# Edge stage of a graph network layer: segment sum in high and low parts, the power on GpSimd, indices made ahead

## The chip, the core and the metric

The kernel runs on one core of a Trainium2 chip. The metric is the device time of one execution in microseconds. Five engines work side by side and meet at semaphores: TensorE (PE, its weight loads as PEld), VectorE (DVE), ScalarE (ACT), GpSimd (POOL) and SyncE (SP), which only issues DMAs here. Each engine takes its instructions in order; a wait holds everything that is queued behind it on that engine.

## The reference

3125 nodes with 256 features, 103125 edges (50000 drawn ones in both directions, and a loop per node), sorted by node. The input is layer-normalized to h, then for every edge

```python
x = concat(h[ei], h[ej], d2)
msg = silu(x @ mW1 + mb1)
msg = layer_norm(msg, ln_g, ln_b)
msg = silu(msg @ mW2 + mb2)
agg = segment_sum(msg, ei, num_segments=3125)
y = silu(concat(h, agg) @ uW1 + ub1) @ uW2 + ub2
```

and behind it, per node, h + y is added to the input, and a feed-forward layer with a routed choice of half of the nodes follows (the node stage, which the change doesn't touch).

## The kernel before

Three stages follow one another, each a block of its own in which all engines start and end together. The first (to about 428 us) sorts edges into 834 tiles of 128 edges, each of which belongs to one of 25 blocks of 125 nodes, and makes `a_sb` (the first layer's part that belongs to the node ei, in a high and a low fp32r part), `b_table` in DRAM (the part of ej, one row per node), and `rec`, a record per edge with the node's place in its block and the neighbour's number in two digits (64 times one plus the other). The third is the node stage (from 1986.84 us).

The edge stage between them works on pairs of tiles: 417 pairs. It is a software pipeline. Slot t of each engine works on pair t in one step, pair t-1 in the next, and so on to pair t-14 (LAST). Six slots are one round; rounds 3 to 68 run as a hardware loop on every engine, those before and behind are written out (`filling`, `draining`).

- **GpSimd**, slot t: two gathers of 128 rows from `b_table` into `g_rows` (L902). It waits for the activation of pair t-6, whose buffer they take (RING is 6), and for the indices that VectorE makes two slots ahead (L1046).
- **SP**, every three slots: `loc_rows` and the lower rows of `ohT` (L877, L880), after TensorE has used the old ones. After the written-out rounds it issues seven loads for the node stage, x among them (L885, L886), before it goes on.
- **VectorE**, slot t, in this order: two additions of `psG` into the block of `agg` of pair t-14 (L1055; the second waits for the first), one-hot `ohT` of pair t-1 (L1139), indices of pair t+2 (L1046), one-hot `ohf` of pair t-12 (L1147), `psH` added to `g_rows` for pair t-2 (L1155), batch statistics of pair t-4 (L1162). Between them, once per three pairs, stand sixteen steps on 6 columns that make the inverse root of the variance by Newton's method and `shift` (L1070 to L1118). At a round's start it loads twelve block numbers into registers (L1042).
- **TensorE**, slot t: `psH` of pair t-2 (L990, fp32r, four matmuls), `psG` of pair t-13 (L999, fp32, the one-hot `ohf` by `msg`), four transposes of `normed` of pair t-10 (L1008), second matmul of pair t-11 into `ps2` (L1016, fp32). One fp32 matmul of 256 columns with 128 rows is two instructions.
- **ScalarE**, slot t: `normed` of pair t-9 (L939, two), Silu of pair t-3 (`act1`, L946), Silu of `ps2` of pair t-12 (`msg`, L951), copy of the transposed ones of pair t-10 (L955).

When GpSimd is through with the gathers it adds h and the bias to x in SBUF (L922, L926, ten instructions).

## Time and profile before

| | |
|---|---|
| median of 3 runs | 2271.79 us (2271.46 to 2272.17) |
| profiled execution: time, span | 2270.75 us, 2268.9 us |
| PE busy | 1973.4 us (87%) |
| DVE busy | 1948.0 us (86%) |
| ACT busy | 1295.1 us (57%) |
| POOL busy | 1035.7 us (46%) |
| gathers (L902) | 834 of 0.948 us |

Times in the views count from the span's start. In a timeline a row is a run of like instructions: its start, its length (up to the end of the last), engine, line, operation, what it writes and reads, the count, and in brackets the idle time of the engine before it with what ended it. Instructions of VectorE overlap: the next one starts before the record of the last ends, so the cost of one is read from start to start. A `q` behind an engine's name marks its sequencer, which issues, waits, branches and loads registers.

### The profile page before, as it was taken

What the parts mean: (1) busy time and instruction counts of PE and PEld (TensorE: products, weight loads), DVE (VectorE), ACT (ScalarE), POOL (GpSimd) and SP (SyncE); (2) the same over time, 40 slices, a digit from 0 to 9 for tenths busy, and PEclk for the clock granted to TensorE, in tenths of its full rate; (3) what the DMA queues carried; (4) which work ended last, traced back from release to release, by engine and by line L of the source; (5) the groups of instructions that cost most, each with busy time, mean ns of one, the idle gap of its engine ahead of it and who ended that gap; (6) DMA issues with size and microseconds to landing.
All of it is one profiled execution on the core that took longest, in us unless ns stands there. A gap on an engine that the chain in (4) does not pass through costs nothing. (4 is left out here: it accounts for less than half of the span.)

```text
span 2268.9 us, 48446 instructions
## 1 busy us (share of the span) xinstructions
PE 1973.4 (87%) x11037; PEld 1678.5 (74%) x11038; DVE 1948.0 (86%) x6373; ACT 1295.1 (57%) x2495; POOL 1035.7 (46%) x1038
## 2 busy tenths in 40 slices
PE   3546674269999999999999999999999997799996
PEld 2324553258888888888888888888888886677775
DVE  5899999659999999999999999999999999746795
ACT  1112331257777777777777777777777775433331
POOL 8753222445555555555555555555555556203000
PEclk9987876579999999999999999999999999899998
DMA  3000000343333333333333333333333333010001
GB/s 123 0 1 21 28 25 18 106 155 91 90 91 97 90 91 97 90 91 97 90 91 97 90 91 97 91 91 97 92 91 97 91 91 73 1 40 2 27 1 57
DMA packets 88779, 164.64 MB, mean 73 GB/s; under 512 B 23133, under 2 KB 59322, under 8 KB 88477
## 3 DMA queue, kind: packets, MB, share of 16 engines
q0 software_dynamic: 42016, 111.40, 18.6%
q1 hardware_dynamic: 45448, 51.78, 7.1%
q10 hardware_dynamic: 1266, 0.83, 0.1%
q8 instruction: 27, 0.44, 0.1%
q14 instruction: 22, 0.18, 0.0%
HBM read 152.30 MB, written 11.65 MB: 72 GB/s over the span
## 5 line engine op out<-in xcount | busy, mean ns | idle before, releaser
L902 POOL DMA_INDIRECT g_rows<-b_table,idx_pair x834 | 790.8, 948 | 704.5 <-DVE idx_pair L1046 566.2
L1016 PE MATMUL ps<-w2g,nT 128*128 128x256 f32 x3336 | 790.8, 380 | 0.0
L1016 PEld LDWEIGHTS ps<-w2g,nT 128*128 128x128 f32 x3336 | 602.9, 191 | 65.0
L939 ACT ACTIVATE normed<-act,shift,rstd_e 128x255 f32<-128x255 f32 x834 | 452.6, 593 | 274.0 <-DVE shift L1118 273.8
L1055 DVE TENSOR_TENSOR agg<-psG,agg 125x256 f32 x834 | 349.4, 419 | 123.3 <-PE psG L999 80.8
L999 PE MATMUL psG<-msg,ohf 128*125 128x256 f32 x1668 | 435.4, 383 | 0.0
L990 PE MATMUL psH<-a_sb,ohT 128*128 x1668 | 344.2, 329 | 67.6 <-issue 47.8
L990 PEld LDWEIGHTS psH<-a_sb,ohT 128*128 128x128 f32 x1668 | 258.6, 192 | 97.4 <-issue 76.1
L946 ACT ACTIVATE act<-g_rows 128x512 f32<-128x512 f32 x417 | 262.8, 630 | 106.1 <-DVE g_rows L1155 94.3
L1162 DVE BATCH_NORM_STATS2 stat_e<-act 128x6 f32<-128x256 f32 x834 | 310.6, 415 | 0.0
L999 PEld LDWEIGHTS psG<-msg,ohf 128*125 128x125 f32 x1668 | 283.7, 187 | 33.9 <-issue 2.2
L1155 DVE TENSOR_TENSOR g_rows<-psH,g_rows 128x512 f32<-128x512 f32 x417 | 284.9, 683 | 6.9 <-DMA g_rows<-b_table,idx_pair 4.7
L955 ACT ACTIVATE nT<-psM 128x512 f32<-128x512 f32 x417 | 247.5, 593 | 56.4 <-PE psM L1008 56.2
L1008 PE MATMUL psM<-identf,normed 128*128 128x128 f32 x1668 | 252.0, 274 | 0.6 <-ACT nT L955 0.6
L951 ACT ACTIVATE msg<-ps 128x512 f32<-128x512 f32 x417 | 241.5, 579 | 5.2 <-PE ps L1016 5.2
L1008 PEld LDWEIGHTS psM<-identf,normed 128*128 128x128 f32 x1668 | 209.6, 141 | 44.1 <-issue 1.3
L1147 DVE TENSOR_TENSOR ohf<-nodes,rec 128x250 f32<-128x250 f32 x417 | 173.4, 416 | 0.0
L1139 DVE TENSOR_SCALAR ohT<-loc_rows,node_col 125x256 fp32r<-125x256 bf16 x417 | 150.3, 361 | 26.4 <-DMA loc_rows<-loc_d 26.1
L512 POOL DMA_INDIRECT rec_d<-recw,dest x62 | 59.7, 962 | 177.5 <-ACT recw L349 83.8
L594 PE MATMUL psK<-oqv,or_ 128*128 128x96 bf16 x806 | 55.7, 232 | 80.6 <-DVE oqv L741 80.6
L349 ACT ACTIVATE recw<-psK 128x96 bf16<-128x96 f32 x62 | 15.4, 250 | 178.4 <-PE psK L594 151.8
L732 DVE TENSOR_TENSOR or_<-x_all,psV 128x1664 bf16<-128x1664 f32 x62 | 116.4, 1877 | 0.0
(200 smaller groups left out, 2150.5 us busy)
## 6 DMA issues: line engine op xcount, KB each, us to landing
loc_rows<-loc_d SPq DMA_DIRECT2D x139, 187.5 KB
g_rows<-b_table,idx_pair POOLq DMA_INDIRECT x834, 2.8
h_sb<-in_x SPq DMA_DIRECT2D x1, 3125.0 KB
b_table<-b_out SPq DMA_DIRECT2D x25, 125.0 KB
x_all<-in_x SPq DMA_DIRECT2D x1, 3125.0 KB
out<-x_all SPq DMA_DIRECT2D x5, 625.0 KB
ohT<-ew_d SPq DMA_DIRECT2D x139, 9.0 KB
rec_d<-rec SPq DMA_DIRECT2D x1, 1668.0 KB, 8.5
```

The source lines that it names most:

```text
L902: pool.indirect_dma_start(g_rows[:, j, n, :], None, b_table[:, :], bass.IndirectOffsetOnAxis(ap=idx_pair[:, j, n:n + 1], axis=0)).then_inc ...
L939: ins = nc.scalar.activation(normed[:, (j - 9) % 2, n, 0:D - 1], act1[:, (j - 9) % RING, n, 0:D - 1], ACT.Identity, scale=rstd_e[:, 1 - fa ...
L946: nc.scalar.activation(act1[:, (j - 3) % RING, :, :], g_rows[:, (j - 3) % RING, :, :], ACT.Silu).then_inc(s_act1, 1)
L951: nc.scalar.activation(msg[:, j % 2, :, :], ps2[:, j % 2, :, :], ACT.Silu).then_inc(s_msg, 1)
L955: nc.scalar.activation(nT[:, j % 2, :, :, :], psM[:, :, :, :], ACT.Copy).then_inc(s_nT, 1)
L990: mm = pe.matmul(psH[:, j % 2, n, :], ohT[:, k, n, :], rows, start=(part == 0), stop=(part == 1))
L999: mm = pe.matmul(psG[0:NB, k, n, :], ohf[:, k, n, :], msg[:, k, n, :], start=True, stop=True)
L1008: mm = pe.transpose(psM[:, n, q, :], normed[:, j % 2, n, q * P:(q + 1) * P], identf[:, :])
L1016: mm = pe.matmul(ps2[:, k, n, :], nT[:, k, n, q, :], w2g[:, q, :], start=(q == 0), stop=(q == 1))
L1055: V.tensor_tensor(room, psG[0:NB, j % 2, n, :], room, ALU.add).then_inc(s_agg, 1)
L1155: V.tensor_tensor(g_rows[:, k, :, :], psH[:, j % 2, :, :], g_rows[:, k, :, :], ALU.add).then_inc(s_hid, 1)
L1162: ins = V.bn_stats(stat[:, q // 3, 2 * (q % 3) + n, :, :].rearrange("p h w -> p (h w)"), act1[:, q, n, :])
```

## The change

- **Segment sum.** `msg` in fp32 is replaced by two fp32r parts. ScalarE writes Silu(`ps2`) as `high` in fp32r, and then Silu(`ps2`) again, in fp32, over `ps2` itself in PSUM; VectorE subtracts to get `low` in fp32r. `psG` is `ohf` (now fp32r) by `high` plus `ohf` by `low`, two matmuls for each tile where there was one fp32 one.
- **Power.** Of the Newton steps five remain, the variance, with `mean2` and `moment` in PSUM. The power -1/2 is one GpSimd instruction (`root`) for three pairs, after the gathers of every third slot, two slots behind the variance; VectorE makes `shift` at the start of the same slot number. ScalarE's steps stand a slot later than before, and so do those behind them; LAST is 15.
- **Indices.** They are made for all tiles at the end of the first stage, three instructions for each of seven groups in place of one copy. In the loop SP copies six columns of them into `idx_ring` for each half round, after the gathers of the round before; the written-out rounds read them in place.
- **Loads.** The seven loads for the node stage are issued by ScalarE, after the written-out rounds, instead of by SP.

```diff
-LAST = 14
+LAST = 15
@@ hand-over
-                    V.tensor_copy(rec[:, g * P:g * P + n, 0:3],
-                                  psR[:, g % 2, :, 0:n].rearrange("p n t -> p t n")).then_inc(s_rec, 1)
+                    link(V.tensor_copy(low_part[:, g * P:g * P + n], psR[:, g % 2, 2, 0:n]))
+                    V.scalar_tensor_tensor(out=idx_all[:, g * P:g * P + n], in0=psR[:, g % 2, 1, 0:n], scalar=64.0,
+                                           in1=low_part[:, g * P:g * P + n], op0=ALU.mult, op1=ALU.add)
+                    V.tensor_copy(loc_e[:, g * P:g * P + n], psR[:, g % 2, 0, 0:n]).then_inc(s_rec, 1)
@@ SP
                         if not has(first, 0):
                             continue
+                        own = bass.ds(2 * first, RING)
+                        if not isinstance(d, int):
+                            for k in range(h * (RING // 2), (h + 1) * (RING // 2)):
+                                sp.wait_ge(s_gather[k], 32 * d)
+                            sp.dma_start(idx_ring[:, h, :], idx_all[:, own]).then_inc(s_idx_in[h], 16)
                         need(sp, s_first, first - RING // 2)
...
                 filling(body)
-                for to, frm in todo:
-                    sp.dma_start(to, frm, allow_slow_non_contiguous=True).then_inc(s_late, 16)
-                sp.dma_start(x_sb[:, :, :], x_v).then_inc(s_xin, 16)
@@ GpSimd
+                def root(d, j):
+                    g, par = (2 * d - 3, 1) if j < 3 else (2 * d - 2, 0)
+                    pool.wait_ge(s_var, 5 * g + 5)
+                    pool.sem_inc(s_apart_pool, 1)
+                    pool.tensor_tensor(rstd_e[:, par, :], var_e[:, par, :], exph[:, 0:6], ALU.pow).then_inc(s_root, 1)
...
                         need(pool, s_act1, t - RING + 1)
-                        pool.wait_ge(s_idx, t + 1)
+                        if not isinstance(d, int) and j % 3 == 0:
+                            pool.wait_ge(s_idx_in[j // 3], 16 * (d - PEEL + 1))
...
+                    if j % 3 == 0 and has(t, 9):
+                        root(d, j)
@@ ScalarE: normed t-10, then
+                    if has(t, 13):
+                        act.wait_ge(s_second, t - 12)
+                        need(act, s_sum, t - 14)
+                        nc.scalar.activation(high[:, (j - 13) % 2, :, :], ps2[:, (j - 13) % 2, :, :], ACT.Silu).then_inc(s_high, 1)
+                    if has(t, 4):
...
-                        nc.scalar.activation(msg[:, j % 2, :, :], ps2[:, j % 2, :, :], ACT.Silu).then_inc(s_msg, 1)
+                    if has(t, 13):
+                        act.wait_ge(s_high, t - 12)
+                        nc.scalar.activation(ps2[:, (j - 13) % 2, :, :], ps2[:, (j - 13) % 2, :, :], ACT.Silu).then_inc(s_msg, 1)
...
                 filling(body)
+                for to, frm in todo:
+                    act.dma_start(to, frm, allow_slow_non_contiguous=True).then_inc(s_late, 16)
+                act.dma_start(x_sb[:, :, :], x_v).then_inc(s_xin, 16)
@@ TensorE
-                        pe.wait_ge(s_msg, t - 12)
-                        pe.wait_ge(s_ohf, t - 12)
+                        pe.wait_ge(s_low, t - 13)
+                        pe.wait_ge(s_ohf, t - 13)
...
-                            mm = pe.matmul(psG[0:NB, k, n, :], ohf[:, k, n, :], msg[:, k, n, :], start=True, stop=True)
+                            pe.matmul(psG[0:NB, k, n, :], ohf[:, k, n, :], high[:, k, n, :], start=True, stop=False)
+                            mm = pe.matmul(psG[0:NB, k, n, :], ohf[:, k, n, :], low[:, k, n, :], start=False, stop=True)
@@ VectorE: the slot after the change
+                    shifts(t, d, j)
                     if has(t, LAST):
                         add(t, j, 0)
-                    step(1)
+                    variance(t, d, j, 1)
+                    variance(t, d, j, 2)
+                    variance(t, d, j, 3)
                     if has(t, LAST):
                         add(t, j, 1)
-                    step(2)
+                    variance(t, d, j, 4)
...
-                    if has(t, 0):
-                        index(t + LEAD, (j + LEAD) % RING)
...
-                    step(8)
+                    if has(t, 13):
+                        dve.wait_ge(s_msg, t - 12)
+                        V.tensor_tensor(low[:, (j - 13) % 2, :, :], ps2[:, (j - 13) % 2, :, :], high[:, (j - 13) % 2, :, :],
+                                        ALU.subtract).then_inc(s_low, 1)
```

## Rows read from the trace of the kernel before

**Rows 1.** Windows: stretch, then busy us (count) of PE, PEld, DVE, ACT, POOL.

```profile
1000.00:1300.00 300.00, 300.00 (x1695) 265.69 (x1695) 274.94 (x1133) 225.89 (x425) 160.85 (x170) 1.00 0.34 94
```

**Rows 2.** Timeline of VectorE, one slot without Newton steps.

```profile
1218.90 0.98 DVE L1055 TENSOR_TENSOR agg<-psG,agg 125x256 f32 x2
1219.80 0.34 DVE L1139 TENSOR_SCALAR ohT<-loc_rows,node_col 125x256 fp32r<-125x256 bf16 x1
1220.06 0.15 DVE L1046 SCALAR_TENSOR_TENSOR idx_pair<-rec 128x2 int32 x1
1220.13 0.41 DVE L1147 TENSOR_TENSOR ohf<-nodes,rec 128x250 f32<-128x250 f32 x1
1220.46 0.68 DVE L1155 TENSOR_TENSOR g_rows<-psH,g_rows 128x512 f32<-128x512 f32 x1
1221.06 0.74 DVE L1162 BATCH_NORM_STATS2 stat_e<-act 128x6 f32<-128x256 f32 x2
1221.72 0.41 DVE L1055 TENSOR_TENSOR agg<-psG,agg 125x256 f32 x1
```

**Rows 3.** Timeline of VectorE, a round's first slot with Newton steps, and its end.

```profile
1200.46 0.41 DVE L1055 TENSOR_TENSOR agg<-psG,agg 125x256 f32 x1
...
1207.61 0.15 DVE L1118 SCALAR_TENSOR_TENSOR shift<-tmp,rstd_e 128x6 f32<-128x6 f32 x1
1208.86 0.99 DVE L1055 TENSOR_TENSOR agg<-psG,agg 125x256 f32 x2 [1.10 <-PE psG L999]
```

**Rows 4.** Source L1042, 1000 to 1300: count, then ns min/median/max.

```profile
L1042 DVEq TENSOR_LOAD <-tile_block x14: 846/850/854, 1016.2 to 1292.7; - x14
```

**Rows 5.** Timeline of TensorE: fp32r psH, fp32 psG, transposes.

```profile
1203.64 0.52 PE L990 MATMUL psH<-a_sb,ohT 128*128 x3
1203.99 1.03 PE L999 MATMUL psG<-msg,ohf 128*125 128x256 f32 x4
1204.86 0.60 PE L1008 MATMUL psM<-identf,normed 128*128 128x128 f32 x4
```

**Rows 6.** Timeline of ScalarE: the Silu of ps2.

```profile
1209.54 0.58 ACT L951 ACTIVATE msg<-ps 128x512 f32<-128x512 f32 x1
```

**Rows 7.** GpSimd: a gather in the timeline, the power in the groups by line.

```profile
1202.72 0.94 POOL L902 DMA_INDIRECT g_rows<-b_table,idx_pair  x1 [0.77 <-DVE idx_pair L1046]
...
L1292 POOL TENSOR_TENSOR rs<-rs,exph 125x5 f32<-125x5 f32 x5 | 5.9, 1176 | 0.4
```

**Rows 8.** Timelines: DMA issues of SP and ScalarE at the start, SP and VectorE near 480.

```profile
2.90 25.93 SPq L252 DMA_DIRECT2D wij<-in_L_gnn_mW  x1
3.22 0.27 ACTq L292 DMA_DIRECT2D a_sb<-in_edge_weight  x1
...
478.50 25.27 SPq L877 DMA_DIRECT2D loc_rows<-loc_d  x1
510.71 0.35 DVE L1139 TENSOR_SCALAR ohT<-loc_rows,node_col 125x256 fp32r<-125x256 bf16 x1 [22.34 <-DMA loc_rows<-loc_d]
```

**Rows 9.** Timelines: VectorE and GpSimd near the end; first work of the node stage.

```profile
1913.67 29.01 DVE L1072 TENSOR_TENSOR tmp<-stat_e 128x6 f32<-128x6 f32 x1
1914.27 14.21 POOL L922 TENSOR_TENSOR x_all<-x_all,h_sb 125x1280 f32<-125x1280 f32 x5
...
1986.84 0.11 POOL L1281 MEMSET epst<- 125x5 f32 x1 [44.20 <-POOLq L784]
```

**Rows 10.** VectorE beside GpSimd: timelines, and source L1462 (ns min/median/max).

```profile
453.45 0.94 POOL L902 DMA_INDIRECT g_rows<-b_table,idx_pair  x1 [0.30 <-issue]
453.96 0.55 DVE L1139 TENSOR_SCALAR ohT<-loc_rows,node_col 125x256 fp32r<-125x256 bf16 x1
...
1201.00 0.95 POOL L902 DMA_INDIRECT g_rows<-b_table,idx_pair  x1 [0.30 <-issue]
1201.43 0.35 DVE L1139 TENSOR_SCALAR ohT<-loc_rows,node_col 125x256 fp32r<-125x256 bf16 x1
...
L1462 DVE TENSOR_SCALAR score<-sc,brb x5: 230/230/1228, 2015.9 to 2087.2; 125x5 f32<-125x5 f32 x5
```

More of the change, by code:

```diff
@@ L957, in body @@
+                    if has(t, 11):
+                        act.wait_ge(s_nx, t - 10)
+                        need(act, s_second, t - 12)
+                        nc.scalar.activation(nT[:, (j - 11) % 2, :, :, :], psM[:, :, :, :], ACT.Copy).then_inc(s_nT, 1)
                 def body(d):
@@ L1052, in add, with variance @@
                     if n == 0:
-                        dve.wait_ge(s_sum, t - 13)
-                    need(dve, s_agg, 2 * t - 28 + n)
-                    V.tensor_tensor(room, psG[0:NB, j % 2, n, :], room, ALU.add).then_inc(s_agg, 1)
-                def newton(t, d, j, n):
-                    if not has(t, 7 + (n > 8)) or j % 3 != 1 + (n > 8):
+                        dve.wait_ge(s_sum, t - LAST + 1)
+                    need(dve, s_agg, 2 * (t - LAST) + n)
+                    V.tensor_tensor(room, psG[0:NB, (j - LAST) % 2, n, :], room, ALU.add).then_inc(s_agg, 1)
+                def variance(t, d, j, n):
+                    if not has(t, 7) or j % 3 != 1:
                         return
@@ L1121, in slot, with shifts @@
+                def shifts(t, d, j):
+                    if not has(t, 9) or j % 3:
+                        return
+                    g, par = (2 * d - 3, 1) if j < 3 else (2 * d - 2, 0)
+                    dve.wait_ge(s_root, g + 1)
+                    V.scalar_tensor_tensor(out=shift[:, par, :], in0=mean2, scalar=-0.5, in1=rstd_e[:, par, :],
+                                           op0=ALU.mult, op1=ALU.mult).then_inc(s_rstd, 1)
                 def slot(t, d, j):
-                    def step(n):
-                        newton(t, d, j, n)
-                        newton(t, d, j, n + 8)
@@ L1170, in body @@
                         slot(d * RING + j, d, j)
-                for t in range(LEAD):
-                    index(t, t)
-                V.tensor_copy(nodes[:, :], iota_n[:, 1:NB + 1]).then_inc(s_nodes, 1)
+                V.tensor_copy(nodes, iota_n[:, 1:NB + 1]).then_inc(s_nodes, 1)
                 dve.wait_ge(s_nodes, 1)
```

191 lines of the change are left out of this document (73 added, 118 removed).

## The prediction

> **What bounds the kernel now.** I read the page first (TensorE 87% busy, VectorE 86%, ScalarE 57%, GpSimd 46%; the edge loop fills the even middle of the forty slices), then one steady stretch by engine. There TensorE is busy all 300 us of 300 and VectorE 274.94 [rows 1]. The averages say "TensorE", so the next view is VectorE's timeline: where are its missing 25 us? A slot (one pair of tiles) without the small Newton steps goes from the first addition into `agg` at 1218.90 to the next at 1221.72, which is 2.82 us, with nothing waited for [rows 2]. Six pairs, one round of the loop, take 1200.46 to 1221.72, 21.26 us, or 3.54 us per pair [rows 2, 3]. The one hole is at the round's end: `shift` starts at 1207.61, the next addition at 1208.86, 1.25 us later, of which `shift` needs 0.07 [rows 3]. The profile names TensorE's psG as releaser, but that had been done; what fills the hole is VectorE's own load of twelve block numbers into registers, 0.85 us in each round [rows 4], with branch and address work around it. So VectorE has no slack: 6 x 2.82 = 16.92, two sets of small steps at 1.58 each (from 1200.46 to 1207.61 plus the 0.07 of `shift` is 7.22 for two slots, less 2 x 2.82), and 1.18 at the boundary give 21.26. TensorE's steps back to back (next part) come to 3.52 a pair, 21.1 for six: it is second by a hair. Both must get shorter for a gain, and VectorE's sum sets how much.
>
> **The change, part by part.**
>
> *TensorE.* An fp32 matmul of 256 columns starts every 0.217 us (four from 1203.99 to 1204.86); the fp32r ones of psH start every 0.117 us (three from 1203.64 to 1203.99) [rows 5]. The four instructions of psG become four fp32r ones: 0.87 becomes 0.47. A pair was psH 0.47, psG 0.87, four transposes of half the columns 0.44 and the second matmul's eight 1.74, together 3.52; it becomes 3.12 us. This takes TensorE off the bound; alone it is worth nothing, because VectorE stays.
>
> *VectorE, per pair.* Out: the index step (0.07, from 1220.06 to 1220.13). In: `low`, PSUM minus SBUF over 512 elements, the same shape as `g_rows`, which takes 0.60 from start to start (1220.46 to 1221.06) [rows 2]. A slot is then 2.82 - 0.07 + 0.60 = 3.35. No cheaper bound exists for 512 elements in this trace; the dear one is its whole duration of 0.68, 0.08 more. Of the sixteen small steps per three pairs five and `shift` stay. Three stand between the two additions, which are 0.56 apart in any case because the second waits for the first, and are covered; the other three cost 0.07 each, 0.21 instead of 1.58.
>
> *VectorE, the boundary.* The last instruction of the round was `shift`, which waits for the step before it, so the sequencer reached the register load late: 1.18 us. Now it is `low`, which waits only for ScalarE's second Silu, done more than a microsecond earlier by the order below, and behind which 0.60 us of work is still queued, with 0.66 of batch statistics before it. Bounds are 0 and the old 1.18; the sequencer did run ahead of the engine in TensorE, where the same 0.85 us load leaves no hole. I take 0.2, plus 0.03 of new bubbles. Six pairs: 6 x 3.35 + 0.42 + 0.23 = 20.75, against 21.26. From about pair 17 to 417 there are 66.7 rounds: 66.7 x (-0.51) = **-34 us**. If the boundary stayed whole it would be +31.
>
> *ScalarE.* It is busy 225.89 of 300, 2.66 per pair [rows 1]; the second Silu adds 0.58 [rows 6], 3.24 of 3.46. It fits, with 0.2 to spare. Batch statistics now want the activation of the same slot, but it ends about 0.9 us into the slot and they start at 2.1. Cost 0 while this cover holds; each tenth beyond it would be 42 us.
>
> *GpSimd and SP.* The gathers lose their wait for the index. A gather pair takes 2.5 us, 7.5 per three pairs, and `pow` takes 1.18 us for 5 columns [rows 7]; for 6 it lies between that and 1.41 in proportion, and I take 1.3: 8.8 of 10.4, so GpSimd is not the bound, and rows are gathered four slots before they are added. SP's copy of the indices waits for the gathers of the previous round and stands ahead of `loc_rows` and `ew`; those gathers land two slots before SP is released by psH, so nothing queued behind it is later. Cost 0.
>
> *The loads moved from SP to ScalarE.* Today SP's `loc_rows` at 478.50 sits 25.27 us behind the load of x, and VectorE waits 22.34 for it [rows 8]. At the kernel's start the same x load held SP's next DMA for 25.93 us while ScalarE issued its own in 0.27 us [rows 8]: the hold is of the queue, not of all queues. So -22.3. ScalarE issues seven DMAs instead, 4.6 us by SP's spacing, of which it was about 1.3 ahead of VectorE: +3.3. Net **-19 us**. Nothing is queued behind x on ScalarE. Bounds: -22 and 0 (if `loc_rows` slows as much beside x).
>
> *The end.* GpSimd adds h and the bias to x in 14.21 us and as much again; a small VectorE step that started 0.6 before them ended only with them, 29.01 long, while the last three one-hots were still to be made [rows 9]. The new GpSimd program reaches these additions only after the last root, whose variance is in slot 421, when VectorE has no one-hot or two-input SBUF instruction left to be held. From slot 415's start (1912.8) the edge stage needed 74.1 us to 1986.84 [rows 9]. Now: three slots of 3.46, one of 3.1, two of 2.8, 2.8 for variance and root make 21.9, then 28.4 of additions, 50.3; VectorE's drain of 17 slots (under 46) ends first. **-24 us.** Bounds -30 and -15.
>
> *Small.* Three VectorE instructions for one in seven hand-over copies, 0.15 to 0.4 us each: +1. `pow` while the gathers set the pace in the fill: +2.
>
> Sum: -34 - 19 - 24 + 3 = -74 on the profiled execution's 2270.75 us (its span is 2268.9, with 1.9 around it): 2196.8. The median shown is 1.0 above it: **2198 us**.
>
> **The rivals.**
>
> *A. `pow` holds the one-hot comparison (slower).* When GpSimd works on SBUF some VectorE instructions stand still. A one-hot that began 0.51 into a gather took 0.55 instead of 0.35 and ended 0.12 after the gather's own end; `score`, 5 columns, took 1228 ns instead of 230 because a 1280-column GpSimd addition was running [rows 10]. `pow` will run every third slot. Where? `low` ends 0.08 into a slot; psG follows 0.3 later; psG, transposes and second matmul take 0.57 + 0.44 + 1.73; their result is read 0.2 after that, 3.3 in all, which is 0.1 before the next slot. The first Silu and the activation take 1.1 together at 0.58 for the first [rows 6]; GpSimd needs 0.77 from release to gather [rows 7], then two gathers take 2.2. The root then begins about 4.1 us into a slot of 3.5, 0.55 into the next one, and ends at 1.9. The one-hot starts there at 0.90. If it is held until 0.12 after `pow` it ends at 2.0 instead of 1.25: 0.75 each, 1.5 per round, +100 us: **2298 us**. It decides on the sign from 0.55 per `pow` (2 x 0.55 x 66.7 = 74). For it: the two rows. Against it: the hold by a gather covers its last part only; those of the loop that began 0.44 into a gather passed unhindered [rows 10], and the long additions move 1280 columns without pause, while `pow` moves 6 and computes. The position can be off by 0.3 either way, but hardly by enough to miss.
> The Trainium skill says, in "SBUF — State Buffer", section "Who interferes with whom", that the port pair which GpSimd shares with VectorE is an exclusive lock held for the whole instruction. By that rule rival A would be the outcome; the `score` row agrees with it, the gather rows agree only for the gather's later part, and no row shows a `pow` beside such an instruction.
>
> *B. The register load stays on the path* (low is released late or the queue is too short): +1.0 per round, +65 us: 2263 us.
>
> *C. The change does less than it says outside the loop*: x beside `loc_rows` starves it as before, or the last additions hold the drain. +19 to +40: 2217 to 2238 us.
>
> **How the numbers follow.** Forecast 0.50; A 0.34; B 0.07; C 0.09. The forecast's own range is 2175 to 2220 (low's 0.08 per pair is +32, half believed; the boundary at 0 is -15; the end ±8). The 8-in-10 range must reach into A, whose delay of 0.5 to 0.9 gives 2265 to 2318: I take 2178 to 2302. About 0.2% (4.5 us) is what a measurement can tell. A is slower nearly always (0.30 of its 0.34, 0.03 within 0.2%), B and C are mostly faster: faster 0.61, same 0.04, slower 0.35.
>
> **What would show it.** Right: a slot near 3.35 on VectorE, no hole over 0.3 at the boundary, psG of 0.47, TensorE with small idle times before psG behind `low`; no 25 us DMA on SP near 480; no VectorE instruction of 29 us at the end, and GpSimd's additions the last work of the edge stage. Wrong: a one-hot of 0.9 to 1.3 us in every third slot (A); a hole of 1 us per round (B). ScalarE idle under 0.1 per slot would mean that it has become the bound.

## The result and the profile after

The changed kernel takes 2301.06 us (2300.81 to 2301.5), the kernel before beside it 2271.62: ratio 1.0131, 95% interval 1.0113 to 1.0148. The forecast was 2198, faster, with 0.50; slower had 0.35. The sign is wrong, the time lies inside the range near its upper end, and it came there by no rival's own mechanism, as follows. The profiled execution is 2300.81 us with a span of 2299.0. Some of the chips of the experiments disturb this program: there the kernel before takes 2291 to 2297 us instead of 2272, and single rounds are 1 to 4 us longer, with holes on ScalarE that nothing in the trace explains ("remote"); the text calls such a chip disturbed.

The windows of the steady stretch, the same columns as in [rows 1]:

```profile
1000.00:1300.00 300.00, 276.25 (x1623) 239.69 (x1622) 272.40 (x815) 256.45 (x488) 193.02 (x190) 1.00 0.31 89
```

TensorE is no longer busy all the time, and neither is VectorE, though a round is longer. So the loop waits somewhere. VectorE's timeline around a round's end, to lay beside [rows 2] and [rows 3]:

```profile
1215.83 0.99 DVE L1079 TENSOR_TENSOR agg<-psG,agg 125x256 f32 x2
1216.74 0.34 DVE L1132 TENSOR_SCALAR ohT<-loc_rows,node_col 125x256 fp32r<-125x256 bf16 x1
1217.00 0.41 DVE L1136 TENSOR_TENSOR ohf<-small,rec 128x250 fp32r<-128x250 f32 x1
1217.33 0.68 DVE L1143 TENSOR_TENSOR g_rows<-psH,g_rows 128x512 f32<-128x512 f32 x1
1217.92 0.74 DVE L1149 BATCH_NORM_STATS2 stat_e<-act 128x6 f32<-128x256 f32 x2
1218.58 0.67 DVE L1154 TENSOR_TENSOR low<-ps,high 128x512 fp32r<-128x512 f32 x1
1220.55 0.16 DVE L1112 SCALAR_TENSOR_TENSOR shift<-small,rstd_e 128x6 f32<-128x6 f32 x1 [1.30 <-issue]
1220.93 0.99 DVE L1079 TENSOR_TENSOR agg<-psG,agg 125x256 f32 x2 [0.21 <-issue]
```

The slot is as forecast: `low` costs 0.60 from its place to the next instruction's (the prediction's 3.35 per slot), and no other instruction is longer. But behind `low`, which ends at 1219.25, VectorE stands for 1.30 us, "issue": nothing in the trace is waited for. The source view of the register load, first of this round, then of the steady stretch (count, ns min/median/max), to lay beside [rows 4]:

```profile
L1071 DVEq TENSOR_LOAD <-tile_block x1: 2733/2733/2733, 1217.7 to 1217.7; - x1
...
L1071 DVEq TENSOR_LOAD <-tile_block x57: 2728/2732/2748, 575.7 to 1815.7; - x57
```

The load takes 2.73 us, where it took 0.85. It starts 1217.70, early, as forecast (the sequencer does run ahead), and still ends at 1220.43, 1.18 after `low`. From the start of one slot to the next (a slot that makes `shift` starts with it) a round is 3.48, 3.33, 3.41, 3.48, 3.34 and 3.41, together 20.45, and then 1.69 at the boundary: 22.14. 56 rounds from 575.7 to 1815.7 give the same 22.14. Before it was 21.26.

Where the 30.1 us of span came from, by the register loads of rounds 3 and 4 and of round 69, and the node stage's first work. Before, the node stage began at 1986.84 [rows 9]; the loads in the source view, before and then after:

```profile
L1042 DVEq TENSOR_LOAD <-tile_block x2: 858/859/860, 483.3 to 527.1; - x2
...
L1042 DVEq TENSOR_LOAD <-tile_block x1: 852/852/852, 1908.8 to 1908.8; - x1
...
L1071 DVEq TENSOR_LOAD <-tile_block x2: 2742/2743/2744, 486.5 to 509.2; - x2
...
L1071 DVEq TENSOR_LOAD <-tile_block x1: 2745/2745/2745, 1948.2 to 1948.2; - x1
```

and in GpSimd's timeline after:

```profile
1992.18 14.30 POOL L936 TENSOR_TENSOR x_all<-x_all,ub2b 125x1280 f32<-125x1280 f32 x5
2015.46 0.10 POOL L1269 MEMSET epst<- 125x5 f32 x1 [8.99 <-POOLq L787]
```

| stretch | before | after | difference |
|---|---|---|---|
| start to round 3 | 483.3 | 486.5 | +3.3 |
| round 3 to 4 (the stall behind x) | 43.9 | 22.7 | -21.2 |
| rounds 4 to 69 (65 rounds) | 1381.7 | 1439.0 | +57.3 |
| round 69 to the node stage | 78.0 | 67.3 | -10.8 |
| node stage | 282.1 | 283.5 | +1.5 |

So two suspects are left by the trace: the load (new and long), which the loop's +57.3 hangs on, and the end, which brought 10.8 of 24. GpSimd's last addition ends at 2006.48 (1992.18 + 14.30), VectorE's last one at 2001.5, but the node stage begins at 2015.46.

### The profile page after: what moved, and what is told of

Read it like the earlier page. It is cut to its first block and busy times, and to the rows that moved or that the text cites. A ratio compares the mean times of both kernels' runs of the same rounds, so it can differ in the third digit from the quotient of the medians.

```text
span 2299.0 us, 46512 instructions
## 1 busy us (share of the span) xinstructions
PE 1910.6 (83%) x11037; PEld 1600.2 (70%) x11038; DVE 1958.9 (85%) x4995; ACT 1501.9 (65%) x2912; POOL 1236.0 (54%) x1177
## 5 line engine op out<-in xcount | busy, mean ns | idle before, releaser
L910 POOL DMA_INDIRECT g_rows<-b_table,idx_ring x792 | 762.1, 962 | 516.3 <-ACT act L960 373.6
L1027 PE MATMUL psG<-high,ohf 128*125 128x256 f32 x834 | 256.0, 329 | 110.8 <-DVE low L1154 93.4
L956 ACT ACTIVATE high<-ps 128x512 fp32r<-128x512 f32 x417 | 249.3, 598 | 76.3 <-PE ps L1045 76.1
L1027 PEld LDWEIGHTS psG<-high,ohf 128*125 128x125 f32 x834 | 154.0, 185 | 187.5 <-issue 176.3
L1154 DVE TENSOR_TENSOR low<-ps,high 128x512 fp32r<-128x512 f32 x417 | 280.3, 672 | 4.5 <-ACT ps L964 4.5
L964 ACT ACTIVATE ps<-ps 128x512 f32<-128x512 f32 x417 | 245.9, 590 | 0.3
L1028 PE MATMUL psG<-low,ohf 128*125 128x256 f32 x834 | 214.8, 281 | 0.0
L899 POOL TENSOR_TENSOR rstd_e<-var_e,exph 128x6 f32<-128x6 f32 x139 | 188.8, 1358 | 23.1 <-DVE var_e L1104 19.9
L1136 DVE TENSOR_TENSOR ohf<-small,rec 128x250 fp32r<-128x250 f32 x417 | 170.3, 408 | 0.0
L1028 PEld LDWEIGHTS psG<-low,ohf 128*125 128x125 f32 x834 | 155.2, 186 | 0.2
```

Of the source, the lines that this page charges most:

```text
L910: pool.indirect_dma_start(g_rows[:, j, n, :], None, b_table[:, :], bass.IndirectOffsetOnAxis(ap=which, axis=0)).then_inc(s_gather[j], 16)
L1027: pe.matmul(psG[0:NB, k, n, :], ohf[:, k, n, :], high[:, k, n, :], start=True, stop=False)
L1028: mm = pe.matmul(psG[0:NB, k, n, :], ohf[:, k, n, :], low[:, k, n, :], start=False, stop=True)
L1154: V.tensor_tensor(low[:, (j - 13) % 2, :, :], ps2[:, (j - 13) % 2, :, :], high[:, (j - 13) % 2, :, :], ALU.subtract).then_inc(s_low, 1)
```

## The experiments

Theory 1: the load is slow because of where it begins. Before it read from word 12d-28 of the table (LAST 14), TensorE's reads from 12d-4, both multiples of four; with LAST 15 it is 12d-30. The rivals: it is slow because of what runs beside it (`pow`, the second Silu, `low` ahead), or the loop is longer for another reason.

**e1_aligned.** The load begins two words earlier and fills 16 registers, so the start and the count change together:

```diff
-                    lo = d * 2 * RING - 2 * LAST
-                    n0, n1 = 0, 2 * RING
+                    lo = d * 2 * RING - 2 * LAST - 2
+                    n0, n1 = 0, 2 * RING + 4
...
-                    b = dve.snap(regs[2 * j + n], min_val=0, max_val=BLOCKS - 1)
+                    b = dve.snap(regs[2 * j + n + 2], min_val=0, max_val=BLOCKS - 1)
```

> The changed kernel, with VectorE's load of block numbers in the loop made to begin two words earlier, at a multiple of four words (12d-32 instead of 12d-30), and to fill 16 registers instead of 12; nothing else differs. Theory (the start word makes the load slow): the load takes 0.85 us, as the loads of 12 registers that begin at a multiple of four words do in both traces, instead of 2.73; it then ends before `low`, which is queued ahead of the round's first addition, so the 1.69 us hole at the round's end goes and six pairs take 20.45 to 20.65 us (the six slots of the changed kernel's trace sum to 20.45). 66.7 rounds x 1.5 to 1.69 is 100 to 113 us: 2188 to 2201 us. Rival 1 (the load is slow because of what runs beside it: `pow` on GpSimd, `low` ahead of it, ScalarE's second Silu): the load stays at 2.7 us or grows, time 2301 or above. Rival 2 (with the hole gone TensorE or ScalarE sets the pace at about 3.46 a pair, as TensorE is busy 3.40 of 3.69 us per pair now): six pairs 20.8, 2212 us.

Measured on a disturbed chip: 2355.7 us, before 2292.9, ratio 1.027 (1.024 to 1.031). The load was 1.107 us, but rounds took 21.7 to 25.0 us. The load got short, but the time is far from the one expected; by itself this run doesn't tell whether the chip or the kernel makes the rounds long.

**e5_aligned_again.** The same kernel.

> The same kernel as e1_aligned, once more beside the kernel before. There the load was shorter (1.107 us for 16 registers, 2.73 for 12 before), the hole at the round's end was 0.3 us (1204.01 to 1204.96 less `shift`), but rounds took anything from 21.7 to 25 us, with holes of 1.5 to 3.8 us on ScalarE ahead of `high` and of `nT` that no instruction in the trace explains; rounds of the kernel before and of the changed kernel were also disturbed on that chip (before 2292.9 instead of 2271.6 us; single rounds of 24 and 25 us among rounds of 21.3). Theory: on a chip whose kernel before takes 2272 us, the disturbance is gone and six pairs take 20.45 to 20.65 us: 2188 to 2201 us. Rival 2 (TensorE or ScalarE sets the pace at 3.46 a pair): 2212 us. Rival 3 (the disturbance comes with the shorter round itself, whatever the chip): 21.7 to 23.2 us per six pairs and 2290 us or more again.

Measured on an undisturbed chip: **2195.05 us** (2194.02 to 2196.42), before 2271.97, ratio 0.966 (0.964 to 0.968). Rivals 2 and 3 fall, and with the load at 1.108 us so does rival 1 of e1. The source view of the load:

```profile
L1071 DVEq TENSOR_LOAD <-tile_block x61: 1103/1108/1115, 571.0 to 1804.7; - x61
```

VectorE's timeline at a round's end:

```profile
1208.55 0.74 DVE L1149 BATCH_NORM_STATS2 stat_e<-act 128x6 f32<-128x256 f32 x2
1209.20 0.67 DVE L1154 TENSOR_TENSOR low<-ps,high 128x512 fp32r<-128x512 f32 x1
1209.80 0.15 DVE L1112 SCALAR_TENSOR_TENSOR shift<-small,rstd_e 128x6 f32<-128x6 f32 x1
1209.93 0.99 DVE L1079 TENSOR_TENSOR agg<-psG,agg 125x256 f32 x2
```

And the windows:

```profile
1000.00:1300.00 300.00, 294.10 (x1754) 259.55 (x1753) 291.58 (x876) 276.96 (x526) 208.65 (x206) 1.00 0.35 97
```

The load (in this round 1208.33 to 1209.43) ends while `low` runs; there is no hole. 60 rounds from 571.0 to 1804.7 are 20.56 each, 1.58 less than in the changed kernel, and 66.7 times that is 105 of the 106 us between the two kernels. Two words of the start address make the difference between 2301 and 2195 us.

**e2_before_off** asks the reverse: the kernel before, nothing of the change, its table two words further.

```diff
-        tile_block = alloc(edge_mem, "tile_block", [1, TG * P], I32)
+        tile_block = alloc(edge_mem, "tile_block", [1, TG * P + 8], I32)
...
-                        dve.reg_load(regs[n0:n1], tile_block[0:1, bass.ds(lo + n0, n1 - n0)])
+                        dve.reg_load(regs[n0:n1], tile_block[0:1, bass.ds(lo + n0 + 2, n1 - n0)])
```

(The DMA that fills the table writes from word 2; TensorE loads 16 registers from a multiple of four.)

> The kernel before, with the table of block numbers stored two words further, so that VectorE's load of 12 registers begins two words off a multiple of four; TensorE's load is kept at a multiple of four (16 registers). Nothing of the change is in it. Theory (start word): VectorE's load takes 2.73 us in the loop instead of 0.85, the hole at the round's end grows by 1.88 from 1.18 to 3.06, six pairs take 23.1 us instead of 21.26, and the time is 2271.6 + 66.7 x 1.88 = 2397 us. Rival (the slow load belongs to something else in the changed kernel): the load stays at 0.85 us, time within 0.3% of before.

Measured 2430.9 us, before 2292.9, ratio 1.060 (1.058 to 1.062). Again as **e12_before_off_again**:

> The same kernel as e2_before_off, where the median round was 23.16 us as expected but single rounds of 24 to 27 us, with the chip's disturbance, stood between. On a chip whose kernel before takes 2272 us: the load of 12 registers from two words off takes 2.73 us, six pairs 23.15 us throughout, and the time is 2272 + 66.7 x 1.89 = 2398 us. Rival: below 2290 us.

Measured 2424.7 us, before 2295.4, ratio 1.057 (1.055 to 1.059): +129 us. Both ran on disturbed chips, so the total has some disturbance in it, but the middle one of e12's rounds is 23.16 us, the 21.26 plus 1.9 expected. The load:

```profile
L1043 DVEq TENSOR_LOAD <-tile_block x53: 2721/2724/2746, 578.6 to 1798.7; - x53
```

With neither `pow` nor a second Silu nor `low` in the program it is 2.72 us. The contention rival falls.

**e3_sizes and e6_sizes** measure the load by itself.

> The changed kernel with 48 more register loads in VectorE's program after its last addition in the edge stage: 1, 2, 4, 6, 8, 12, 14 and 16 registers, each from words 200, 201, 202, 203, 204 and 206 of the table. Theory: four neighbouring words that begin at a multiple of four are fetched as one, others one by one. From the traces (12 from 2 words off: 2.73 us; 6 from word 0: 1.06; 12 and 8 from a multiple of four: 0.85 and 0.84) a single costs about 0.17 and the rest 0.73, so 16 registers from 200 or 204 should take 0.86 us, from 201, 202, 203 or 206 about 3.4; 4 registers 0.8 or so against 1.4; 1 or 2 registers the same from all starts. If only the even starts mattered, 202 and 206 would be fast and 201 and 203 slow; if only the count mattered, no start would differ. Rival (contention): here no other engine works beside most of these loads, so all should be 0.85 us or less.

Its trace shows none of the 48 loads (nothing used their registers), so it tells only the changed kernel's time on a disturbed chip (2331.9 us, one execution, before 2292.9).

> The kernel of e5_aligned_again with 48 more register loads in VectorE's program after its last addition in the edge stage: 1, 2, 4, 6, 8, 12, 14 and 16 registers, each from words 200, 201, 202, 203, 204 and 206 of the table, each followed by one small VectorE instruction that uses the last register (in e3_sizes nothing used the registers and the loads were dropped when the program was built). Theory: words are fetched in groups that must begin at a multiple of four, others one by one. 12 registers from 200 or 204: 0.85 us; from 202 or 206: 2.73; 16 from 200 or 204: 1.107, as in e1_aligned; 1 or 2 registers alike from every start. If only evenness counted, 202 and 206 would be as fast as 200. Rival (contention with TensorE, GpSimd or ScalarE makes it slow): nothing works beside these loads, so none exceeds 1.1 us.

The source view, one line per load; by the source L1203 and L1205 load 4 registers from word 200 and 201, L1239 to L1247 load 12 from 200, 201, 202, 203 and 204, L1263 and L1267 load 16 from 200 and 202:

```profile
L1203 DVEq TENSOR_LOAD <-tile_block x1: 356/356/356, 1902.8 to 1902.8; - x1
...
L1205 DVEq TENSOR_LOAD <-tile_block x1: 959/959/959, 1903.4 to 1903.4; - x1
...
L1239 DVEq TENSOR_LOAD <-tile_block x1: 851/851/851, 1927.5 to 1927.5; - x1
...
L1241 DVEq TENSOR_LOAD <-tile_block x1: 2718/2718/2718, 1928.6 to 1928.6; - x1
...
L1243 DVEq TENSOR_LOAD <-tile_block x1: 2722/2722/2722, 1931.5 to 1931.5; - x1
...
L1247 DVEq TENSOR_LOAD <-tile_block x1: 853/853/853, 1937.5 to 1937.5; - x1
...
L1263 DVEq TENSOR_LOAD <-tile_block x1: 1110/1110/1110, 1958.6 to 1958.6; - x1
...
L1267 DVEq TENSOR_LOAD <-tile_block x1: 3601/3601/3601, 1963.8 to 1963.8; - x1
```

| registers | 1 | 2 | 4 | 6 | 8 | 12 | 14 | 16 |
|---|---|---|---|---|---|---|---|---|
| from 200 or 204, us | 0.31 | 0.53 | 0.36 | 0.82 | 0.61 | 0.85 | 1.33 | 1.11 |
| from 201, 202, 203 or 206, us | 0.30 | 0.52 | 0.96 | 1.40 | 1.84 | 2.72 | 3.16 | 3.60 |

Off a multiple of four words (16 bytes) each register costs 0.22 after a first 0.30. On one, four together cost 0.36, each further four 0.25, and a rest of two goes one by one. Evenness doesn't help. From four registers on no other engine works beside these loads: GpSimd's last addition ends at 1901.20. Theory 1 stands in all of it; its sizes did not: e1 took 0.85 for 16 registers and e3 0.8 for four on a multiple of four, and they are 1.11 and 0.36.

**e10_lag16, e13_lag16_again, e17_lag16_third**: one constant, so that the start word is 12d-32 with 12 registers as before.

```diff
-LAST = 15
+LAST = 16
...
                     if has(t, 13):
+                        need(dve, s_sum, t - 14)
                         V.tensor_tensor(ohf[
```

> The changed kernel with LAST = 16 instead of 15 (and the wait that one-hot then needs for TensorE's sum of two pairs before, done long before): VectorE adds one slot later, and its load of 12 registers begins at 12d-32, a multiple of four, with no register more. Theory (start word): the load takes 0.85 us, the hole goes, six pairs take 20.45 to 20.6 us; one slot more in the drain is +3.4: 2195 + 3 = 2198 us where before is 2272. Rival 1 (it is the number of registers or the 16-register form that helped in e5_aligned_again): the load stays at 2.73 us, 2301 us. Rival 2 (TensorE's psG now waits for the addition just begun and gets late): load 0.85 but six pairs 21 or more, 2230 us or more.

> The same kernel as e10_lag16, once more. There the load of 12 registers took 0.856 us from 12d-32, as expected of the start word, but the rounds stood at 21.3 or, after a disturbance, at 23.2 us, with TensorE's psG waiting for VectorE's addition (81 of 300 us), on a chip whose kernel before took 2295 instead of 2272 us. Theory (the late addition holds psG, which is only two buffers deep): undisturbed rounds are 21.3 us throughout, 0.8 more than with 16 registers and the lag of 15, so 2195 + 0.77 x 66 + 3 = 2249 us. Rival 1 (the waits are the chip's disturbance only): 20.5 us per six pairs, 2198 us. Rival 2 (both costs are the kernel's own): rounds at 23.2 us again, 2350 us.

> The same kernel as e10_lag16 and e13_lag16_again (LAST = 16), for a chip whose kernel before takes 2272 us. Theory (start word alone makes the load 0.85 us, but psG behind the late addition costs 0.8 a round): rounds of 21.3 us, 2249 us. Rival 1 (only the start word matters): 20.5 us, 2198 us. Rival 2 (the kernel locks into rounds of 23.2 us by itself): 2350 us or more.

The first two were disturbed: 2349.9 (before 2295.4) and 2370.8 us (before 2294.1), most rounds at 23.2. The third was not: 2248.3 us, before 2271.6, ratio 0.989 (0.987 to 0.992), the 2249 expected. Its load in the source view:

```profile
L1071 DVEq TENSOR_LOAD <-tile_block x59: 852/856/859, 573.9 to 1812.3; - x59
```

From its waits, 1000 to 1300 (us in total, times, longest):

```profile
PEld psG L1027 <- DVE agg L1079: 32.2, 84, 0.9
```

The start word alone brings the load back to 0.856 us, and the kernel becomes 53 us faster than the changed one. The rest of the 106 is taken back by TensorE's psG, whose weight load now waits in nearly every slot (84 times in 300 us) for an addition just begun: 58 rounds from 573.9 to 1812.3 are 21.35 each.

**e8_two_roots** tests rival A of the prediction, `pow` beside the one-hot. The trace of the changed kernel speaks against it already: GpSimd's timeline has two roots in a round:

```profile
1205.31 1.36 POOL L899 TENSOR_TENSOR rstd_e<-var_e,exph 128x6 f32<-128x6 f32 x1
...
1216.33 1.36 POOL L899 TENSOR_TENSOR rstd_e<-var_e,exph 128x6 f32<-128x6 f32 x1
```

The source view of VectorE's one-hot, 1000 to 1300:

```profile
L1132 DVE TENSOR_SCALAR ohT<-loc_rows,node_col x82: 340/345/351, 1000.5 to 1298.5; 125x256 fp32r<-125x256 bf16 x82
```

The one-hot of 1216.74 (shown above) begins 0.41 into a `pow` and lasts 0.34. The position was forecast right (0.35 into it), the hold was not there in any of 82.

```diff
                     pool.tensor_tensor(rstd_e[:, par, :], var_e[:, par, :], exph[:, 0:6], ALU.pow).then_inc(s_root, 1)
+                    pool.tensor_tensor(spare[:, par, :], var_e[:, par, :], exph[:, 0:6], ALU.pow).then_inc(s_spare, 1)
```

> The changed kernel with the `pow` of each root made twice, the second into a spare tile that nobody reads: GpSimd works 1.36 us longer beside VectorE in every third slot. Theory (`pow` of 6 columns holds nothing on VectorE): the one-hot stays at 0.35 us, six pairs at 22.14, time within 0.3% of the changed kernel's (2301 us where before is 2272; ratio to before 1.013). Rival A of the prediction (`pow` holds VectorE's one-hot until 0.12 us after its end): the one-hot meets one of the two in every third slot and is 0.9 to 1.7 us long, at least +100 us: 2400 us or more.

Measured 2306.9 us, before 2272.0, ratio 1.015 (1.014 to 1.017): 5.8 us more than the changed kernel. Two roots in its timeline of GpSimd:

```profile
1208.90 1.37 POOL L901 TENSOR_TENSOR rstd_e<-var_e,exph 128x6 f32<-128x6 f32 x1
1210.24 1.33 POOL L902 TENSOR_TENSOR spare<-var_e,exph 128x6 f32<-128x6 f32 x1
```

The one-hot beside them, in VectorE's timeline:

```profile
1210.21 0.38 DVE L1135 TENSOR_SCALAR ohT<-loc_rows,node_col 125x256 fp32r<-125x256 bf16 x1
```

Over 1000 to 1300 the longest one-hot of this run is 0.48. Rival A is refuted: 2.7 us of `pow` cost a round 0.02 (22.16), and about 4 of the 5.8 us lie in the written-out rounds, where the gathers set the pace. The Trainium skill says in "SBUF — State Buffer", section "Who interferes with whom", that the port pair which VectorE shares with GpSimd is held for the whole instruction. `pow` on 6 columns doesn't show this: the one-hot of 1216.74 ran to its end inside one.

**e4_before_loads** takes one part of the change alone, the seven loads issued by ScalarE.

> The kernel before, with only this part of the change: the six loads of node weights and the load of x are issued by ScalarE instead of SP, after its peeled rounds. Prediction's term: VectorE's wait of 22.3 us for `loc_rows` goes and 3.3 us of issue come, -19 us: 2253 us; in the trace of the changed kernel the three rounds around it were 21.2 shorter and 3.3 longer, -17.9. Rival (x beside `loc_rows` starves it, or the drain takes it back): 2268 to 2272 us.

Measured on a disturbed chip 2274.8 us, before 2292.9, ratio 0.992 (0.990 to 0.994): -18.0, against -19 in the sum. The sign of the term and about its size are borne out; its two parts are looked at below. SP's timeline, where [rows 8] had the issue of 25.27 us:

```profile
478.29 0.26 SPq L867 DMA_DIRECT2D loc_rows<-loc_d  x1
478.59 0.32 SPq L870 DMA_DIRECT2D ohT<-ew_d  x1
488.94 0.28 SPq L867 DMA_DIRECT2D loc_rows<-loc_d  x1
```

What did ScalarE's issue cost? In the changed kernel's trace it begins at 486.46, where the +3.3 of the table's first row has already been lost. That row is `pow` in the written-out rounds: each root stands between the gathers, which run back to back there, and VectorE waits for the roots. The first line is ScalarE's issue in the timeline, the second is from VectorE's waits, 440 to 483 (before has no such wait):

```profile
486.46 0.95 ACTq L986 DMA_DIRECT2D uw<-in_L_gnn_uW  x2
...
DVE shift L1112 <- POOL rstd_e L899: 8.8, 3, 3.6
```

With two roots (e8) that stretch ends 2.2 us later still (round 3 starts at 488.7). What the issue costs is seen in the row behind it, round 3 to 4: 0.6 us over an ordinary round in the changed kernel (22.7 less 22.14), 0.7 in e4 (22.0 less 21.3), 2.0 in e5 (22.6 less 20.56), where before it was 22.6 over (43.9 less 21.26).

**e9_root_only, e14_root_again, e18_root_third** take the root alone: nine of the sixteen steps go, GpSimd makes `pow` behind its gathers, all else as before.

```diff
-                    elif n == 7:
...
+                    elif n < 16:
+                        return
                     else:
-                        dve.wait_ge(s_newton, done + 15)
+                        dve.wait_ge(s_root, g + 1)
```

> The kernel before with one part of the change alone: of the sixteen small VectorE steps per three pairs, the nine of the square root's iteration go and GpSimd takes `pow` of the variance, behind its gathers; sums, indices, lag and loads stay. Theory of the prediction (VectorE and TensorE are bounds a hair apart, 21.26 and 21.1 us per six pairs): VectorE gets nine steps of 0.1 shorter twice per round, 19.5 us, but TensorE's four psG of 0.87 stay, so six pairs take 21.1 us and the loop gains 10 us: about 2262 us, VectorE then waits for TensorE. Rival 1 (VectorE alone was the bound): six pairs 19.5 us, 2155 us. Rival 2 (`pow` holds VectorE's one-hot): six pairs 21.3 or more, 2272 us or above.

> The same kernel as e9_root_only, once more. There most rounds took 22.0 to 22.1 us, longer than the 21.3 of the kernel before, and the stall of 29 us in the drain was gone (rounds of 20.7 and 19.2 instead of 48.4), on a chip whose kernel before took 2295 us. Theory 1 (the longer round is the kernel's own: GpSimd's root, put behind the gathers without a slot more of lag, makes `shift` and the activation late): 22.05 us again, 2272 + 0.8 x 66 - 29 = 2296 us. Theory 2 (disturbance; TensorE at 21.1 us is the bound as predicted): 2272 - 10 - 29 = 2233 us.

> The same kernel as e9_root_only and e14_root_again (the kernel before with the root on GpSimd alone). Both ran on chips whose kernel before takes 2294 to 2295 us, with unexplained holes ahead of ScalarE's `msg` and `nT` in them (17 to 37 of 300 us), so that rounds of 22.1 us could be the kernel's or the chip's. For a chip whose kernel before takes 2272 us. Theory 1 (disturbance only; TensorE at 21.1 us is the bound, as the prediction has it): six pairs 21.1 us, and the 29 us stall of the drain gone: 2233 us. Theory 2 (the kernel's own): 22.05 us a round, 2296 us. Rival (VectorE alone was the bound): 19.5 us a round, below 2160 us.

All three fell on disturbed chips: 2312.8, 2316.1 and 2332.4 us, before 2295.4, 2294.1 and 2293.4, ratios 1.008 (1.007 to 1.010), 1.010 (1.008 to 1.011) and 1.017 (1.016 to 1.019). A round takes 22.0 to 22.3 on the average. The windows of e14, the same columns as in [rows 1], and the waits of e18, 1000 to 1300:

```profile
1000.00:1300.00 300.00, 289.30 (x1641) 256.96 (x1640) 246.21 (x851) 218.47 (x408) 196.02 (x192) 1.00 0.32 90
...
DVE g_rows L1136 <- PE psH L1000: 37.6, 20, 3.5
ACT msg L961 <- PE ps L1026: 25.2, 10, 3.6
ACT nT L965 <- remote: 21.1, 12, 4.1
```

What this shows: nine steps fewer on VectorE alone brought no gain on these chips. The 2155 us of a kernel that only VectorE bounds is far off: VectorE is busy 246 of 300 us instead of 275, TensorE 289, and VectorE now waits for TensorE, 37.6 of 300 us, as the prediction's "second by a hair" wants it. What stays open: why the round is a whole microsecond above TensorE's 21.1. The unexplained holes (21.1 of 300 us and more) are large enough for it. But nearly every round of e9 and e14 takes 22.0 to 22.2, while in e4, also on a disturbed chip, most take 21.2 or 21.3, so a cost of the kernel's own (theory 1 of e14) is not excluded; the wait for the root itself is small, 0.8 of 300 us in e18. On an undisturbed chip this kernel was not seen.

**The end.** GpSimd's last drain ends 8.7 us after its last addition in the trace of before, of after, of e5 and of e7. It was taken apart in **e7_aligned_end** (e5 with GpSimd's additions divided, three behind the root of slot 417, three behind that of 420, four at the end), in **e11_drain** (e5 with a drain of GpSimd behind the root of slot 417, where it is idle) and in **e15_drain_two** and **e16_drain_two_again** (that drain, and two additions behind the root of slot 420). The edit of e11:

```diff
                     if j % 3 == 0 and has(t, 9):
                         root(d, j)
+                    if isinstance(t, int) and t == PAIRS:
+                        pool.drain()
```

> The kernel of e5_aligned_again with one thing more: GpSimd's ten additions of h and of the bias to x no longer all follow the last root; three stand after the root of slot 417, three after that of slot 420, the other four after the last one. In the changed kernel the node stage began at 2015.46 us, 9 us after GpSimd's last addition by the trace and 14 after VectorE's last one (2001.5); GpSimd's drain (22.97 us) ended at 2015.22 and let it go. Theory: GpSimd's additions and drain are the end of the edge stage; with four instead of ten left (11.6 + 9 us after 1977.8 is 1998) VectorE's last addition becomes the end, -13 us against e5_aligned_again. Rival (the additions hold VectorE's instructions for their whole length, as a small step was held for 29 us in the kernel before): what is gained at the end is lost in front of it, up to 17 us: -13 to +4 us.

Measured 2185.8 us, before 2272.0, ratio 0.962 (0.960 to 0.964): -9.2 against e5, between theory and rival. The node stage begins at 1900.31 instead of 1910.08, but VectorE's last addition is 5.2 us later than in e5, because the additions do hold it. VectorE's timeline beside the first and the last of those in front:

```profile
1854.99 1.60 DVE L1144 TENSOR_SCALAR ohT<-loc_rows,node_col 125x256 fp32r<-125x256 bf16 x1
1859.66 2.73 DVE L1144 TENSOR_SCALAR ohT<-loc_rows,node_col 125x256 fp32r<-125x256 bf16 x1
1873.63 2.27 DVE L1104 TENSOR_TENSOR delta<-stat_e 128x6 f32<-128x6 f32 x1
```

The 0.35 us one-hot lasts 2.73 beside an addition of 1280 columns, though it lasts 0.34 beside a `pow`: here the hold of [rows 9] and [rows 10] is seen again.

> The kernel of e5_aligned_again with one GpSimd drain more, right after the root of slot 417, where GpSimd has nothing to do for 8.7 us; its drain at the stage's end stays. In four traces that last drain ended 8.74 or 8.75 us after GpSimd's last addition (before 1942.65 to 1951.40, changed kernel 2006.48 to 2015.22), but the drain behind the five additions of the node stage only 0.08 after them. Theory 1 (a GpSimd drain that follows gathers costs about 9 us once, the node stage has none): the new drain takes it in the idle time, the last one ends with the last addition, and the node stage begins 8.7 us earlier: 2195 - 8.7 = 2186 us. Theory 2 (it belongs to the additions, or to every drain there): the last drain still ends 8.7 us after the last addition; 2195 us, or up to 9 more if the new one delays the next root.

Measured on a disturbed chip 2232.2 us, before 2295.4, ratio 0.972 (0.970 to 0.974); its time can't be set beside e5's, its trace can. The source view of e5's drain:

```profile
L787 POOLq DRAIN  x1: 22953/22953/22953, 1886.9 to 1886.9; - x1
```

And of e11's, the new one, then the stage's last:

```profile
L916 POOLq DRAIN  x1: 10130/10130/10130, 1897.6 to 1897.6; - x1
...
L787 POOLq DRAIN  x1: 14306/14306/14306, 1932.3 to 1932.3; - x1
```

In e5 the drain ends at 1909.84, 8.74 after the last addition (1901.10). In e11 the early one ends 8.74 us after the root it stands behind (1898.97 to 1907.72), and the last one 0.08 after the last addition (1946.53 to 1946.61). So the 8.7 us come once, with the first drain behind gathers, and not with the additions: theory 1. That it is the gathers is inferred: every such drain had gathers ahead of it, and the node stage's, which has none, ended 0.08 us after the last addition. Nor is 8.7 a fixed price. The first stage's drain stands behind indirect writes and ended 5.2 us after the last of them, in the traces of before and after alike.

> The kernel of e11_drain (GpSimd's early drain after the root of slot 417), and of GpSimd's ten additions two stand behind the root of slot 420, the others behind the last one. In e11_drain the last drain ended 0.08 us after the last addition (1946.53 to 1946.61) and the node stage began 6.3 us after VectorE's last drain; two additions fewer at the end are 5.8 less. Theory: GpSimd's and VectorE's work end together, and the node stage begins about 14 us earlier than in e5_aligned_again: 2181 us where before is 2272 us (e7_aligned_end: 2186). Rival (the two additions hold VectorE's steps by as much): 2186 us, as with the early drain alone.

> The same kernel as e15_drain_two, once more: aligned load, GpSimd's early drain, two of its ten additions behind the root of slot 420. Theory: on a chip whose kernel before takes 2272 us the rounds are 20.5 us throughout and the time is 2181 us (14 less than e5_aligned_again). Rival (the early drain or the two additions are paid for in front of the end): 2186 us or more.

The first was disturbed (2234.8 us, before 2294.1, ratio 0.974). The second was not: **2182.2 us** (2180.91 to 2182.43), before 2271.6, ratio 0.960 (0.958 to 0.962), the 2181 expected. GpSimd and VectorE end together:

```profile
1887.61 8.65 POOL L937 TENSOR_TENSOR x_all<-x_all,ub2b 125x1280 f32<-125x1280 f32 x3
1896.59 0.10 POOL L1283 MEMSET epst<- 125x5 f32 x1 [0.33 <-POOLq L787]
```

This is the best of the kernels that ran, 89 us under the one before and 119 under the changed one.

## Why the prediction was wrong, point by point

**What bounds the kernel: right as far as it was seen.** VectorE had no slack, and a shorter VectorE alone (e9, e14, e18) gained nothing, though only on disturbed chips. Once the load is mended, TensorE is busy 294 and VectorE 292 of 300 us: the two are still a hair apart.

**TensorE, VectorE's slot, ScalarE, GpSimd, SP: right where it counts.** 20.45 for six slots stand against a forecast of 20.52 without the boundary (6 x 3.35 + 0.42). ScalarE fits (256 busy in 300), and GpSimd waits for the activation, not for indices. The four instructions of psG take 0.57 from start to start in e5 instead of 0.47; TensorE had room for it.

**The boundary: this is the step that failed.** The prediction put it at 0.2 (0.23 with new bubbles) with bounds of 0 and the old 1.18, because it took the duration of the load, 0.85, as given and asked only whether it would be hidden. The reason for the cover was right: the load does start 1.55 before `low` ends. But the change moved the load's first word (LAST from 14 to 15 moves it by two), and its duration went to 2.73. With 0.85 in its place the cover would have been ample; with 1.11 it was (e5). The term came to 1.69, 1.46 more than taken; the slots, 0.07 a round shorter than taken, give a little back. So a round was forecast 0.51 shorter and came 0.88 longer: over the table's 65 rounds 90 of the 104 us between the sum's 2196.8 and the measured 2300.81. The end (below) is another 13. The upper bound was unfounded too: the old 1.18 belonged to a load at the other start, and nothing asked what in the instruction's operands the change touched. The place was rival B's; its price (+1.0 a round) was too small and its reason (a late release, a short queue) wrong.

**The loads moved: right in kind and nearly in size.** -19 stood in the sum and -18.0 came alone (e4). By the traces of before, after and e5 the stall's -22.3 came to -22.6 and the +3.3 for ScalarE's issue to 0.6 to 2.0, a net of about -21; why e4's time shows 3 us less, on a disturbed chip, stays open. The +3.3 of the table's first row is another term, the "small" one: `pow` in the fill, for which the sum had +2, and +1 more for the hand-over. That it equals the forecast for the issue is a coincidence.

**The end: right in kind, sized wrong.** -24 was forecast, bounds -30 and -15; it came to -10.8. Counted from slot 415's start it took 60.9 us instead of 50.3: the slots up to the last root 23.2 instead of 21.9, the additions 28.7 as taken, and then 9.0 that the sum didn't have. They stood in the trace before, but under cover: the drain (source view below) ended at 1951.4, 8.7 after the last addition and 35 us before the node stage. The change took that cover away. The remaining 2.4 is slot 414 with its long load.

```profile
L784 POOLq DRAIN  x1: 22873/22873/22873, 1928.5 to 1928.5; - x1
```

**The rivals.** A is refuted: its place in the slot was right, the hold did not exist for a `pow`, so its price was never put to the test. C is not borne out as it was priced: outside the loop the sum had -40 us (loads, end and small) and the table has -29, 11 short where C has 19 to 40, and of its two reasons (`loc_rows` starved, the additions holding VectorE's drain) neither was there. The 2301 near A's 2298 is a coincidence, and so is that it lies inside the range: the range reached that far for A's sake.

**What would show it.** The list held the right row, "a hole of 1 us per round" (it was 1.69), and gave it to B alone.

That e5, with the load mended, takes 2195.05 where 2198 was forecast, does not make the rest exact: the loop came out better (its register loads of rounds 4 and 69 start at 509.4 and 1845.4, 45.7 less than before, against -34, since the boundary is 0.1 and not 0.2 and the slots are 0.07 less), and the end worse (-13.3 against -24).

## What to carry to other kernels

When a constant moves, follow it into every address that is worked out from it, and ask of each instruction that reads there whether its duration may hang on the start. A duration out of the trace holds for the operands it was seen with. And when a change makes another engine the last one to finish a stage, count that engine's whole tail, its drain too; look for it in the trace before, under the work that used to hide it.

## What the runs showed of the hardware

- A register load from SBUF takes 0.85 us for 12 registers that begin at a multiple of four words (e6_sizes, and the rounds of the kernel before, e10, e13 and e17), 2.72 us from the other starts (e6_sizes, and the rounds of e2, e12 and the changed kernel). The Trainium skill, in "Runtime: NRT & Kernel Launch", section "Instruction fetch mechanics", gives about 200 ns per register even for bulk loads, stated there for loads from HBM; here it holds for loads off a multiple of four (0.22 each), and the measured 0.85 for 12 on one is a third of it.
- A drain of GpSimd that is the first behind gathers ended about 8.7 us after the instruction ahead of it (before, after, e5, e7, e11); a second one, with two roots and ten additions between (e11), 0.08. Why was not looked into.
- `pow` of 6 columns on GpSimd didn't hold VectorE's one-hot (0.34 to 0.35 us in all 82 of 300 us); beside additions of 1280 columns the same one-hot lasted up to 2.73 us (e7).
